# Two of the four DMAs that swap a rotated chunk's sine half issued by ScalarE instead of SyncE

## What is computed

```python
for i in range(6):
    x = attn_layer(shift_tokens(x), Wqkv[i], q_scale[i], k_scale[i], Wo[i]) + x
    x = ffn_layer(shift_tokens(x), ln_g[i], ln_b[i], W1[i], b1[i], W2[i], b2[i]) + x

# in attn_layer, 16 heads of 64 features, q and k each 1024 wide
q = l2norm(q) * qs
k = l2norm(k) * ksc
q = q * cos * scale + rotate_half(q) * sin * scale
k = k * cos * inv   + rotate_half(k) * sin * inv
# then softmax over windows of 32 queries and 64 keys, times v, times Wo
```

## Time and profile before

| | before |
|---|---|
| time, median of 3 runs | 2294.89 us (2286.56 to 2439.66) |
| the profiled execution's own time | 2313.61 us |
| its span, first to last instruction | 2311.9 us |
| PE busy | 2061.6 us (89%) |
| DVE busy | 1622.5 us (70%) |
| ACT busy | 911.6 us (39%) |
| POOL busy | 922.6 us (40%) |
| mean granted clock of PE | 0.931 of full speed |
| DMAs t<-t issued by SP at L427 | 1536 |

### The profile page before, as it was taken

How to read it: one execution, slowest core, us unless ns; L and a number is a source line. 1 busy time by engine, 2 the same in 40 slices (tenths; PEclk the granted TensorE clock), 3 DMA queues, 4 the chain that set the end, 5 groups by cost and what they waited for, 6 DMA issues and landing times.

```text
span 2311.9 us, 48227 instructions
## 1 busy us (share of the span) xinstructions
PE 2061.6 (89%) x20232; PEld 920.0 (40%) x20232; DVE 1622.5 (70%) x2739; ACT 911.6 (39%) x1388; POOL 922.6 (40%) x726
## 2 busy tenths in 40 slices
PE   5999948999999999899999999999999998999984
PEld 2334333344434434343444344433434443444332
DVE  5455455777677767867877778678768777786753
ACT  2344411353345335443434353344335434543430
POOL 2122213543454344435434544354344435443520
PEclk9799866999999999999999999899999999999977
DMA  2200002311322122223213321232132133212200
GB/s 54 72 11 10 1 5 70 92 47 38 101 65 68 46 72 73 61 52 101 52 38 96 74 70 46 62 88 61 41 98 53 46 87 74 58 45 56 70 5 19
DMA packets 104046, 131.55 MB, mean 57 GB/s; under 512 B 28530, under 2 KB 48144, under 8 KB 103824
## 3 DMA queue, kind: packets, MB, share of 16 engines
q1 hardware_dynamic: 103828, 128.46, 22.0%
HBM read 24.54 MB, written 1.05 MB: 11 GB/s over the span
## 4 chain that ended last, share of the span: by engine, by line
PE 52%; DVE 24%; POOL 9%; SPq 5%; ACT 4%; DMA 3%; issue 3%; POOLq 0%; DVEq 0%; ACTq 0%
PE ps_z L1065 11%; PE ps_r L983 8%; SPq L427 4%; DVE t L724 4%; PE ps_s L1041 4%; PE ps_z L1016 4%; PE ps_z L991 4%; POOL prob L500 3%; POOL prob L496 3%; DMA t<-t 3%; PE ps_z L1058 3%; DVE sinv L756 2%; DVE prob L752 2%; DVE t L657 2%; PE ps_r L1093 2%
## 5 line engine op out<-in xcount | busy, mean ns | idle before, releaser
L724 DVE TENSOR_TENSOR t<-ps_r,rot 128x1024 f32<-128x1024 f32 x384 | 461.5, 1211 | 209.6 <-PE ps_r L983 151.2
L983 PE MATMUL ps_r<-xs,w_qk_sb 128*128 128x512 f32 x768 | 430.4, 643 | 96.8 <-ACT sq L552 96.7
L552 ACT ACTIVATE sq<-ps_r 128x512 f32<-128x512 f32 x384 | 229.0, 596 | 499.9 <-DVE t L724 497.1
L490 POOL TENSOR_TENSOR q_hat<-t 128x512 f32<-128x512 f32 x192 | 243.6, 1270 | 322.0 <-DMA t<-t 322.0
L1065 PE MATMUL ps_z<-z,vo 128*128 128x512 f32 x768 | 350.0, 599 | 2.2 <-ACT z L574 2.2
L490 POOL TENSOR_TENSOR k_hat<-t 128x512 f32<-128x512 f32 x192 | 243.6, 1273 | 266.0 <-DMA t<-t 265.8
L496 POOL TENSOR_TENSOR prob<-prob,rnorm 128x1024 f32<-128x1024 f32 x96 | 182.7, 1903 | 375.5 <-DVE prob L752 375.5
L574 ACT ACTIVATE z<-ps_z 128x512 f32<-128x512 f32 x384 | 213.4, 601 | 201.2 <-PE ps_z L1058 200.0
L983 PEld LDWEIGHTS ps_r<-xs,w_qk_sb 128*128 128x128 f32 x768 | 122.5, 192 | 318.4 <-ACT sq L552 217.8
L1041 PEld LDWEIGHTS ps_s<-k_hat,q_hat 64*32 64x32 f32 x12288 | 199.7, 115 | 91.1 <-issue 91.1
L1041 PE MATMUL ps_s<-k_hat,q_hat 64*32 64x64 f32 x12288 | 232.6, 230 | 0.0
(11 more groups left out here) (171 smaller groups left out, 2546.7 us busy)
## 6 DMA issues: line engine op xcount, KB each, us to landing
t<-t SPq DMA_DIRECT2D x1536, 64.0 KB, 2.0
rot<-in_dram SPq DMA_DIRECT2D x12, 512.0 KB, 4.6
w_qk_sb<-in_dram SPq DMA_DIRECT2D x24, 256.0 KB, 3.0
w_vt_sb<-in_dram SPq DMA_DIRECT2D x6, 512.0 KB, 4.2
w_o_sb<-in_dram SPq DMA_DIRECT2D x6, 512.0 KB, 5.0
z<-q_hat SPq DMA_DIRECT2D x128, 16.0 KB
w_sb<-in_dram SPq DMA_DIRECT2D x6, 341.0 KB
x_tok<-in_dram SPq DMA_DIRECT2D x4, 256.0 KB, 3.7
```

Source lines behind the costliest of these rows:

```text
L490: nc.gpsimd.tensor_tensor(dst, t12[:, slot, 0, :], t2[:, slot, :], ALU.add).then_inc(added.sem, 1)
L552: nc.scalar.activation(sq[:, n % SQ_SLOTS, :], ps_r[n % 2][:, :], ACT.Square).then_inc(squared.sem, 1)
L724: nc.vector.tensor_tensor(t12[:, slot, :, :], ps_r[n % 2][:, :].unsqueeze(1).to_broadcast([P, 2, SEQ]), rot[:, n // PAIRS, :, :], ALU.mult ...
L983: nc.tensor.matmul(ps_r[n % 2][:, :], w_qk_sb[:, n, :], xs[:, seq, WIN:WIN + SEQ], start=True, stop=True).then_inc(projected.sem, 1)
```

## The change

Of the four DMAs of a chunk, the first two (r = 0 and 1, partitions 0 to 63) stay on SyncE. The other two (r = 2 and 3, partitions 64 to 127) are issued by ScalarE, in the step "square", after its wait for the rotation and ahead of its wait for the sums and ahead of the square itself. Sizes, addresses, the semaphore and its count stay as they are.

```diff
@@ swap, SyncE
                 sp.wait_ge(rotated.sem, rotated.at(u, c))
-                for r in range(4):
+                for r in range(2):
                     there = r + 1 - 2 * (r % 2)
                     sync.dma_start(t2[WIN * there:WIN * (there + 1), slot, :],
                                    t12[WIN * r:WIN * (r + 1), slot, 1, :]).then_inc(swapped[slot].sem, 16)
@@ step, ScalarE
                 if kind == "square":
                     act.wait_ge(rotated.sem, rotated.at(u, n))
+                    for r in range(2, 4):
+                        there = r + 1 - 2 * (r % 2)
+                        nc.scalar.dma_start(t2[WIN * there:WIN * (there + 1), n % T_SLOTS, :],
+                                            t12[WIN * r:WIN * (r + 1), n % T_SLOTS, 1, :]).then_inc(swapped[n % T_SLOTS].sem, 16)
                     act.wait_ge(summed.sem, summed.at(u, (n - SQ_SLOTS) // 4) if n >= SQ_SLOTS else summed.at(u - 1, 2 + n // 4))
                     nc.scalar.activation(sq[:, n % SQ_SLOTS, :], ps_r[n % 2][:, :], ACT.Square).then_inc(squared.sem, 1)
```

## The result

The changed kernel takes 2457.5 us (median of 4 runs, 2441.3 to 2470.0). The kernel before took 2286.6, 2294.9 and 2317.7 us; a fourth run of 2439.7 us was in a slower state that some executions show, and is left out of the ratio. The ratio is 1.068, with an interval of 1.056 to 1.081. The forecast was slower, 2375 us, inside a range of 2290 to 2530. The direction, the place and the size of the issue's price were right; the amount, 3.5%, was about half of what came. The time lies outside the forecast's own band (2345 to 2430) and inside the one that was given to the rival "shared generation" (2430 to 2600, chance 0.18).

A forecast was written before the change was run, and what follows sets the result against it. PE's list was taken to bound the kernel; 1.0 us a unit won from SP against ACT's issues delaying squares left 3.35 us, over 24 units 80 us, so 2295 + 80 = 2375 us, range 2290 to 2530.

The forecast's parts named there:

- the forecast's own band: Whole kernel: an issue pair at about 1.2 us, with or without overlap, gives 2345 to 2430 us; chance 0.58.
- shared generation: Rival: both issuers share the descriptor generator, square waits up to 2.5 us instead of 1.2; about 2570 us, chance 0.18.
- the loop rotation, issues, square, project: First part of a unit: rotation, square, project two chunks on, rotation; each turn gets 1.2 us longer.
- Chunks 12 to 15 have slack: Second part: squares 12 to 15 have slack behind 3.6 us output projection blocks; nothing more lost.
- the price of an issue: On ACT ahead of the square: 2 × 0.6 = 1.2 us a chunk, taken from SP's issue of the same DMA.
- the idle time that this puts ahead of the projects: PE's idle time before L983, put down to the square, rises from 3.7 us a unit to about 7.
- milder overlap: Weaker form of the shared-generation rival: values between, from 2430 us on, within that rival's 0.18.
- the walk: One unit moved step by step through four engine lists: square 11 late by 3.3 us, project 13 by 3.35.
- PE's clock falls: Sign that the forecast is wrong: PE's clock, 1.00 in the profiled unit, falls.
- the forecast's 3.35: Loss in us a unit, reached at project 13; 24 units × 3.35 = 80 us.
- the relief: SP loses two issues a chunk, so add 0 starts sooner and the exp about 1.0 us earlier a unit.
- the pair ahead of the square: ACT's two issues before each square, 4.35 us a unit in the walk: 3.35 plus 1.0 set against it.

The follow-up runs named there:

- the kernel without SyncE's issues: Changed kernel with SyncE's two swap DMAs dropped, ScalarE's two kept ahead of the square, half the swap left out; ratio to the kernel before 1.047.
- the relief alone: Kernel before with SyncE issuing only two of the four DMAs and ScalarE none, half of the swap left out; ratio 0.980.
- The two kernels in the middle: Both omit half the swap of the kernel before: SyncE issuing two and ScalarE none, 0.980; ScalarE issuing two ahead of the square and SyncE none, 1.047.
- The kernel with the added work: Kernel with ScalarE's issues ahead of the square for chunk 11 only (1.020), plus six unused PE matmuls ahead of project 13; ratio to the kernel before 1.010.

## Why the prediction was right and wrong

**Right: the kind of loss and its place.** The loss comes through the loop rotation, issues, square, project. With the square first it is gone (0.996). The part up to square 11 grew and the second did not (43.54 us in the mean of units 1 to 22, before and after). Chunks 12 to 15 have slack (1.0015).

**Right: the price of an issue.** Taken from SyncE's row, 1.2 us a pair; alone on ScalarE it is 1.16. Right, too, was the idle time that this puts ahead of the projects, about 7 us a unit foretold and 7.4 measured.

**Wrong: "shared generation" was priced at nothing in the sum.** The rival had 1.3 us a pair. It is 0.25 us a pair (1.41 against 1.16), on ScalarE's side alone, and the kernel without SyncE's issues is 48 us faster. The rival had also named milder overlap with times from 2430 us on. The measured 2457 us lies in that band, but the 48 us are too few to have brought it there: the kernel without them has a ratio of 1.047, some 2410 us. The row that hinted at it, 0.59 us for issues in a row against 0.51 for the shortest, had been read. A small share of it belonged into the forecast's own sum: 0.25 us on a loop that loses more than it is delayed.
The Trainium skill, "Perfetto Trace Analysis", section "DMA Instruction — HWDGE (DVE, Sync)", has the wait for the generator's lock inside the issue's reported duration. A second issue of ScalarE's that takes 0.87 us beside SyncE's and 0.61 alone agrees with it; that it is this lock was not shown here.

**Wrong: a link of the walk was left out.** It moved the exp behind square 0 by the issues, but left rotation 2 where it was. The timeline of DVE, first of the kernel before, then of the changed one (L760 is the sum over that exp's output):

```profile
1048.97 1.20 DVE L756 TENSOR_REDUCE sinv<-prob 128x16 f32<-128x1024 f32 x1
...
1052.11 1.21 DVE L724 TENSOR_TENSOR t<-ps_r,rot 128x1024 f32<-128x1024 f32 x1
```

```profile
1174.14 1.22 DVE L760 TENSOR_REDUCE sinv<-prob 128x16 f32<-128x1024 f32 x1 [0.70 <-ACT prob L573]
...
1177.29 1.21 DVE L728 TENSOR_TENSOR t<-ps_r,rot 128x1024 f32<-128x1024 f32 x1
```

From rotation 0 (1044.96 and 1169.36) the sum comes at 4.01 and 4.78 us, rotation 2 at 7.15 and 7.93: 0.8 us later. DVE ran without a gap from there to rotation 2, so it had no slack to take this up. With square 2's own 1.45 us, project 4 came 2.2 us late, a project that the walk doesn't name; PE had a gap of 2.4 us, and the clock was low behind it. The walk had project 6 late by 0.8 us. In the traces it is at 15.21 us from rotation 0 before (1060.17) and at 17.77 after:

```profile
1187.13 1.13 PE L987 MATMUL ps_r<-xs,w_qk_sb 128*128 128x512 f32 x2 [0.89 <-ACT sq L556]
1189.72 1.13 PE L987 MATMUL ps_r<-xs,w_qk_sb 128*128 128x512 f32 x2 [1.46 <-ACT sq L556]
...
1199.15 3.59 PE L1069 MATMUL ps_z<-z,vo 128*128 128x512 f32 x8
```

(These are projects 6 and 7 and the first output block.) Output 0 went from 25.22 to 29.79, so 4.6 us late instead of 2.1. From there to square 11 these two units differ by another 1.45 us, the walk had 1.2. In the mean of units 1 to 22 rotation 2 is 1.1 us late, project 4 2.6, project 6 3.4, output 0 5.5 and square 11 6.3, so 5.5 of the 6.3 us are there at output 0.

**Wrong, and the largest term: PE's work was priced at its length of before.** "PE's clock falls" was named as a thing that would prove the forecast wrong, and then nothing was put down for it. PE's busy time in the first part grew by 2.4 us a unit, at a mean granted clock of 0.931 instead of 0.987. That is most of the 3.0 us a unit by which the forecast's 3.35 fell short of 6.3; idle time alone, 3.9, was near it. (It is a split of the time and not of its causes: a longer matmul can also fill time in which PE would have waited.) The one unit that was walked had a clock of 1.00 in both parts, so its rows could not show it; in the kernel before, 16 of units 1 to 22 are below 1.00 in one part or the other. At project 13 filling the gap brought the clock back to 1.00 in every unit.

**Wrong: the relief.** 1.9 us a unit instead of 1.0. The walk gave only what the chain had through chunk 0. That part is borne out in the mean of units 1 to 22: add 0 starts 5.8 us after rotation 0 begins before, 4.9 in the changed kernel and 4.2 with the relief alone, where project 6 comes 1.2 us earlier. In the unit that was walked and the one after the change it doesn't show (5.8 us and 6.1). The rest of the relief comes behind project 6, 1.7 us in sum at square 11; by which link was not followed.

In sum, against the kernel before: relief −46 us (−24 forecast), the pair ahead of the square +155 us (+104), SyncE's issues and transfers beside it +48 us (0). The forecast's make 80. Ours make 157 us, the measured 0.068, but they must: they are the steps from one kernel to the next, so the sum confirms nothing. The two kernels in the middle move half of the data, and by the intervals the three terms are open by some 15, 20 and 30 us.

## What to carry to other kernels

A DMA issue on a compute engine is an instruction of 0.5 to 0.9 us in its list, and its price is set by what stands behind it there, not by the engine's idle share: the same change costs 6.8% with the issues ahead of the square and nothing on balance with them behind it. Put the instruction that others wait for first and the issue second, and move only as many issues as the crowded queue has to lose; here one in four gave 1.2%, two in four gave 0.4%. When a delay is followed through the lists by hand, follow everything behind the late instruction, across engines that have no gap, and don't take PE's durations as fixed if the delay opens gaps of 2 us in its work. And walk a typical unit: the one walked here was the shortest, with other loads in the queue and a clock that most units don't have.

## What the runs showed of the hardware that was not expected

- Beside SyncE's issues ScalarE's take a little longer: 1.41 us for a pair of 64 KB DMAs instead of 1.16. SyncE's pair stays at 1.14. Landing takes 2.2 us from ScalarE's queue at the median in the changed kernel, 2.0 from SyncE's.
- An issue on ScalarE runs beside an activation that was started ahead of it: in the kernel with the square first the issue starts at 1189.54 and the square at 1189.53. It holds up only what is behind it.
- PE's mean granted clock was 0.77 in the 7.3 us behind a gap of 2.2 us, between the levels of 1.2 and 2.4 GHz; with six small matmuls in the gap it was 1.00. Of 22 units 13 had such a drop behind gaps of 1.76 us or more, and none with the gap filled. The kernel with the added work was 1.0% faster, though its clock over the second part was no higher (0.946 against 0.947).
